# Latent projections ahead of the channel mixing in an attention and FFN kernel

## The chip, the cores and the metric

One core of one Trainium2 chip. The metric is the time of one execution on the device in microseconds, as the median of repeated runs. The profile is of one further execution.

## What is computed

`x` has shape (128, 32, 512): 128 samples, 32 channels, 512 time steps, in float32. The part of the reference that the change touches is the beginning:

```python
h  = einsum('bct,bcd->bdt', x, weights[condition])     # 16 sets of 32x32 channel weights
q_c = h @ Wq_c.T + bq_c                                # 192 latent features from 512 steps
kv  = h @ Wkv_c.T + bkv_c                              # 64 + 64 features
...                                                    # 32 heads, softmax over the 32 channels of a sample
x  = x + out                                           # then a gated convolution over time and a dequantised FFN
```

The channel mixing works on the channels of one sample, and the projection on its time steps. The two are linear and act on different axes, so they may be done in either order.

## The kernel before, in words

Five engines run instruction streams written out by hand and joined by semaphores. A queue runs strictly in the order of its code. The samples come in `NS` = 8 groups of 16, numbered 0 to 7 here (`k`). 16 samples of 32 channels make `ST` = 512 tokens. Each group is taken through two units `u` = 2k and 2k+1, one for each half of the 32 heads. In a unit, PE multiplies the latents by folded head weights (`fold`, L730, 64 rows in each half of the array), ACT takes the result to `qt`, PE makes the scores (L774), DVE and ACT do the softmax (`take_scores`, `below_max`, `soft`, `normalised`), and PE applies the probabilities (`values`, L797) and the value weights (`output`, L598 to L600).

The exact matmuls are built of three matmuls of type fp32r: a value is split into a rounded `high` part and a `low` rest, and `three` (L598 to L600) sums high*high, high*low and low*high. The split costs ACT a cast and DVE a subtraction. A few matmuls are plain fp32; each of them stands as two records in the trace.

A new group begins at the end of each odd unit, and this is the place of the change. `mixed_x(i)` (L616) mixes the channels of eight samples: the stationary operand is a tile of `x` (tokens by 128 time steps), the moving one a 128x128 block diagonal matrix `mix` of four samples' channel weights, in plain fp32, with the result laid out by time. It runs twice for a group, 16 matmuls of 128 columns. ACT and DVE split the result into `h_high` and `h_low` (`mixed_high`, `mixed_low`). Then `project_ca`, `project_ab` and `project_kv` each make 4 x 3 fp32r matmuls of 512 columns with the weights `wcT_high` and `wcT_low` as the stationary operand. ACT and DVE take the results out with their biases (`projected_ca`, `projected_ab`, `projected_kv`), and copies of 64 rows make the third latent tile `q_high[1]` and `q_low[1]`. PE's order there is output part 0, both `mixed_x`, output parts 1 and 2, the three projections, output part 3, and then `fold` of the next unit.

In units 1, 3 and 5 DVE has further work between these steps: `angles(first, last)`, steps of the convolution's angle computation on tiles of 512 elements (L1463 to L1484, `o_sum` in the trace). Seven of them stand beside each of the groups 1, 2 and 3, and none beside groups 4 to 7.

At the very start, DVE builds selection matrices (`chooser`) from the conditions, and PE makes the first channel weights from them (L915), and it turns the projection weights (L928), since `gather`, the indirect load of channel weights on POOL's queue, would come later. POOL's gathers serve group 1 onwards there.

## Time and profile before

| | us |
|---|---|
| median of 3 runs | 772.38 (770.73 to 773.88) |
| the profiled execution | 769.3 |
| its span in the profile | 767.5 |
| PE busy | 751.7 (98%) |
| DVE busy | 618.5 (81%) |
| ACT busy | 380.0 (50%) |
| POOL busy | 200.3 (26%) |

The profiled execution is 3.1 us below the median, and 1.8 us of it lie outside its span. Busy time on PE is counted while a matmul is in the array, with its fill and drain, so neighbouring matmuls overlap: what one costs is read from the distance between starts, and not from its duration. In the timeline the columns are start, duration, engine, line, operation, tiles and shape, and in brackets the idle time before and what ended it.

### The profile page before, as it was taken

What the parts mean: (1) busy time and instruction counts of PE and PEld (TensorE: products, weight loads), DVE (VectorE), ACT (ScalarE), POOL (GpSimd) and SP (SyncE); (2) the same over time, 40 slices, a digit from 0 to 9 for tenths busy, and PEclk for the clock granted to TensorE, in tenths of its full rate; (3) what the DMA queues carried; (4) which work ended last, traced back from release to release, by engine and by line L of the source; (5) the groups of instructions that cost most, each with busy time, mean ns of one, the idle gap of its engine ahead of it and who ended that gap; (6) DMA issues with size and microseconds to landing.
All of it is one profiled execution on the core that took longest, in us unless ns stands there. A gap on an engine that the chain in (4) does not pass through costs nothing.

```text
span 767.5 us, 18485 instructions
## 1 busy us (share of the span) xinstructions
PE 751.7 (98%) x7769; PEld 613.4 (80%) x7769; DVE 618.5 (81%) x1109; ACT 380.0 (50%) x675; POOL 200.3 (26%) x203
## 2 busy tenths in 40 slices
PE   9999999999999999999999999999999899999996
PEld 7777686978788787869787786978677699999996
DVE  5676899998998796777769776878889688888887
ACT  2475546546563675655465546545655322222221
POOL 5002020020002010270200000000040788888872
PEclk9999999999999999999999999999999999999999
DMA  9920010010001000000200010002207268888861
GB/s 223 229 76 5 2 59 3 1 59 3 2 2 59 2 1 29 1 4 14 87 1 2 2 56 2 1 2 59 84 2 187 69 142 209 200 208 204 205 132 70
DMA packets 42739, 51.74 MB, mean 67 GB/s; under 512 B 7025, under 2 KB 29601, under 8 KB 42657
## 3 DMA queue, kind: packets, MB, share of 16 engines
q1 hardware_dynamic: 40384, 49.87, 26.0%
q8 instruction: 62, 1.02, 0.6%
q0 software_dynamic: 1056, 0.49, 0.3%
q10 hardware_dynamic: 1216, 0.19, 0.2%
q14 instruction: 21, 0.16, 0.1%
HBM read 41.91 MB, written 8.63 MB: 66 GB/s over the span
## 4 chain that ended last, share of the span: by engine, by line
PE 92%; DVE 6%; ACT 1%; issue 1%; POOL 0%; DVEq 0%
PE ps L730 33%; PE ps L598 9%; PE ps L599 8%; PE ps L600 8%; PE ps L774 6%; PE ps L797 4%; PE ps L1087 4%; PE ps L616 4%; PE ps L1088 4%; PE ps L1056 2%; PE ps L693 1%; PE ps L1044 1%; PE ps L1046 1%; PE ps L1045 1%; PE ps L1070 1%
## 5 line engine op out<-in xcount | busy, mean ns | idle before, releaser
L1188 ACT ACTIVATE qt<-ps,m_bias 128x512 f32<-128x512 f32 x228 | 145.8, 686 | 97.0 <-PE ps L730 97.0
L730 PE MATMUL ps<-q_high,m_high 64*128 64x512 f32 x768 | 165.3, 397 | 0.5 <-issue 0.5
L730 PE MATMUL ps<-q_high,m_low 64*128 64x512 f32 x768 | 161.6, 387 | 0.0
L730 PE MATMUL ps<-q_low,m_high 64*128 64x512 f32 x768 | 113.8, 387 | 0.0
L730 PEld LDWEIGHTS ps<-q_high,m_high 64*128 64x128 f32 x768 | 88.9, 184 | 15.7 <-issue 6.2
L730 PEld LDWEIGHTS ps<-q_high,m_low 64*128 64x128 f32 x768 | 89.1, 184 | 8.9
L1450 DVE TENSOR_TENSOR z_low<-ps,z_high 128x512 fp32r<-128x512 f32 x128 | 79.5, 680 | 13.8 <-ACT z_high L1206 13.8
L730 PEld LDWEIGHTS ps<-q_low,m_high 64*128 64x128 f32 x768 | 81.3, 184 | 9.9
L528 POOL TENSOR_TENSOR o_sum<-o_part,o_part 128x512 f32<-128x512 f32 x7 | 9.1, 1304 | 288.5 <-ACT o_part L1216 288.5
L1193 ACT ACTIVATE sc<-sc 128x512 f32<-128x512 f32 x60 | 38.0, 633 | 76.3 <-DVE sc L1435 76.2
L1206 ACT CAST z_high<-ps 128x512 fp32r<-128x512 f32 x128 | 66.7, 597 | 12.3 <-PE ps L797 8.0
L1377 ACT COPY x1T_far<-ps 128x128 f32<-128x128 f32 x32 | 8.5, 267 | 103.7 <-PE ps L1056 103.7
L774 PE MATMUL ps<-qt,kv 128*32 128x512 f32 x480 | 55.0, 595 | 0.9 <-DVE z_low L1450 0.5
L598 PE MATMUL ps<-z_high,wvT_high 128*128 128x512 f32 (+1 forms) x132 | 53.5, 405 | 0.0
L599 PE MATMUL ps<-z_low,wvT_high 128*128 128x512 f32 (+1 forms) x132 | 51.0, 386 | 0.8 <-issue 0.8
L584 POOL TENSOR_TENSOR x_s<-x,fb 128x512 f32<-128x512 f32 x32 | 43.5, 1360 | 31.2 <-DVE x L1758 31.2
L600 PE MATMUL ps<-z_high,wvT_low 128*128 128x512 f32 (+1 forms) x132 | 50.7, 384 | 0.0
L1456 DVE TENSOR_SCALAR qt<-ps,m_bias 128x512 f32<-128x512 f32 x28 | 20.9, 749 | 35.1 <-PE ps L730 35.0
L1443 DVE TENSOR_TENSOR sc<-sc,row_stat 128x512 f32<-128x512 f32 x60 | 44.3, 738 | 2.1
L1445 DVE STREAM_TRANSPOSE pT<-sc 128x512 f32<-128x512 f32 x60 | 42.7, 712 | 2.0
L1435 DVE TENSOR_TENSOR sc<-sc,row_stat 128x512 f32<-128x512 f32 x60 | 41.6, 693 | 2.1
L576 POOL TENSOR_TENSOR x_s<-x_s,bo 128x512 f32<-128x512 f32 x32 | 41.9, 1310 | 0.0
(294 smaller groups left out, 1652.7 us busy)
## 6 DMA issues: line engine op xcount, KB each, us to landing
x_in<-in_x SPq DMA_DIRECT2D x16, 512.0 KB, 3.7
x_s<-in_x SPq DMA_DIRECT2D x32, 256.0 KB, 5.5
out<-res SPq DMA_DIRECT2D x31, 256.0 KB, 3.3
toep_high<-taps_scratch SPq DMA_DIRECT2D x32, 192.0 KB, 4.2
toep_low<-taps_scratch SPq DMA_DIRECT2D x32, 192.0 KB, 4.8
toep_far<-taps_scratch SPq DMA_DIRECT2D x32, 64.0 KB, 5.5
wq_nope<-in_L_attn_Wq_up SPq DMA_DIRECT2D x2, 768.0 KB, 10.8
wq_nope<-in_L_attn_Wq_up SPq DMA_DIRECT2D x1, 1536.0 KB, 18.1
```

Source lines behind the costliest of these rows:

```text
L576: pool.tensor_tensor(x_s[c % RX][:], x_s[c % RX][:], bo[:], ALU.add).then_inc(s["xb_done"], 1)
L584: pool.tensor_tensor(tiles(x_s[c % RX]), backwards(x1[c % 2]), tiles(fb), ALU.add).then_inc(s["x1b_done"], 1)
L598: pe.matmul(out, lh, rh, start=start, stop=False)
L599: pe.matmul(out, lh, rl, start=False, stop=False)
L600: return pe.matmul(out, ll, rh, start=False, stop=stop)
L730: mm = pe.matmul(ps[:, fold_bank(u, j) + e, :], weights[rows, (GH * g + j) // 2, c, :], moving[c][rows, :], start=start, stop=stop)
L774: mm = pe.matmul(ps[32 * b:32 * b + 32, SBANK[n], :], kv[:, tok], qt[:, :, tok], start=True, stop=True)
L1188: act.activation(qt[:, j, :], ps[:, fold_bank(u, j) + j % 2, :], ACT.Identity, bias=m_bias[:, h:h + 1]).then_inc(s["qt_done"], 1)
L1206: act.copy(z_part(z_high, m_, b), z_made(u, m_, b)).then_inc(s["zh_done"], 1)
L1443: dve.tensor_tensor(rows(n), rows(n), wide(n), ALU.mult).then_inc(s["norm_done"], 1)
L1445: dve.transpose(flat(pT[:, n]), flat(sc[:, n])).then_inc(s["turn_done"], 1)
L1450: dve.tensor_tensor(z_part(z_low, m_, b), z_made(u, m_, b), f(z_part(z_high, m_, b)), ALU.subtract).then_inc(s["zl_done"], 1)
```

## The change

Projection and mixing change places. `x` is given to the kernel laid out by time as well (`x_groups`: for each group, 128 partitions by 4 tiles of time by 512 tokens), and the projection weights are given transposed (`wcT`). ACT rounds the loaded `x` to `x_high`, and DVE makes `x_low`. `project(k)` then takes a tile of 128 tokens as the stationary operand and 320 columns of projection weights as the moving one, so for 4 token tiles, 4 time tiles and 3 products there are 48 fp32r matmuls of 320 columns. The 320 columns are all features once. ACT copies each result to `feat` in two pieces, the 320 columns and 64 of them a second time (`feat_taken`). `mix_features(k)` mixes over the channels: the stationary operand is 64 rows (two samples) of 128 features, the moving one 64 columns of channel weights, in plain fp32; for 3 parts, 4 token tiles and two row halves there are 24 matmuls, each half with a bank of its own. It waits for all four of `feat_taken`. The latents come out as before, in halves of a bank pair, and `kv` is taken out a unit later than before, after the third pair of latents.

At the start the selection matrices, their matmuls and the transposed weights go; `project_first` runs as the tiles of `x` arrive, and POOL gathers the channel weights of group 0 too, ahead of the small loads of the convolution's parameters.

```diff
+    x_low = [t(f"x_low{n}", [P, 2, ST], F32R, at=at) for n, at in enumerate((x_at, h_at + 4 * KB))]
+    x_raw = [t(f"x_raw{n}", [P, 2, ST], at=at) for n, at in enumerate((x_at, h_at + 4 * KB))]
+    x_high = t("x_high", [P, TT, ST], F32R, at=qt_at + 16 * KB)
+    feat = t("feat", [P, 4, 64 + FEAT], at=qt_at + 24 * KB)
...
+    mix = t("mix", [P, 4, 64], at=mix_at)
...
+    FEAT_BANK = (BS, BS + 1, BT + 1, BT)
...
+    def mixed_in(part):
+        if part == 0:
+            both = ps[:, BS:BS + 2, 0:256]
+        else:
+            both = ps[:, BZ:BZ + 2, 256 * (part - 1):256 * part]
+        return both
...
+            for tt in range(TT):
+                sp.dma_start(wcT_raw[:, tt, :], d["wcT"][:, tt, :]).then_inc(wc_in[tt], 16)
+                sp.dma_start(half_tile(x_raw, tt), d["x_groups"][0, :, tt, :]).then_inc(x_loaded[tt], 16)
...
+            def masked(k):
+                if k >= 1:
+                    pool.wait_ge(s["kv_ready"], k)
+                for j in range(2):
+                    pool.wait_ge(gather_in[j], 32 * (k + 1))
+                    pool.tensor_tensor(mix[:, 2 * j:2 * j + 2, :].rearrange("p g (b e) -> p g b e", b=2),
+                                       gathered[j][:].unsqueeze(2).broadcast_to([P, 2, 2, C]),
+                                       half_of[:].unsqueeze(1).unsqueeze(3).broadcast_to([P, 2, 2, C]),
+                                       ALU.mult).then_inc(s["mix_ready"], 1)
+            pool.wait_ge(s["row_ready"], 1)
+            gather(0)
+            gather(1)
...
+            def projected(k, n, tt, low):
+                left = half_tile(x_low, tt)[:, P * n:P * n + P] if low else x_high[:, tt, P * n:P * n + P]
+                out_n = ps[:, FEAT_BANK[n], 0:FEAT]
+                if low:
+                    return pe.matmul(out_n, left, wcT_high[:, tt, :], start=False, stop=(tt == TT - 1))
+                pe.matmul(out_n, left, wcT_high[:, tt, :], start=(tt == 0), stop=False)
+                return pe.matmul(out_n, left, wcT_low[:, tt, :], start=False, stop=False)
+            def project_first():
                 for tt in range(TT):
...
+                    pe.wait_ge(s["wcT_done"], tt + 1)
+                    pe.wait_ge(s["xh_done"], tt + 1)
+                    for n in range(4):
+                        projected(0, n, tt, False)
+                    pe.wait_ge(s["xl_done"], tt + 1)
+                    for n in range(4):
+                        mm = projected(0, n, tt, True)
+                        if tt == TT - 1:
+                            mm.then_inc(s["feat_ready"], 1)
+            def project(k):
+                u = 2 * k - 1
+                for n in range(4):
+                    if n != 2:
+                        pe.wait_ge(s["s_taken"], 4 * u + (1, 2, 0, 4)[n])
+                    else:
+                        pe.wait_ge(s["zl_done"], 8 * (u - 1) + 6)
+                    for tt in range(TT):
+                        if n == 0:
+                            pe.wait_ge(s["xh_done"], 4 * k + tt + 1)
+                        projected(k, n, tt, False)
+                    for tt in range(TT):
+                        if n == 0:
+                            pe.wait_ge(s["xl_done"], 4 * k + tt + 1)
+                        mm = projected(k, n, tt, True)
+                    mm.then_inc(s["feat_ready"], 1)
+            def mix_features(k):
+                pe.wait_ge(s["feat_done"], 4 * k + 4)
+                pe.wait_ge(s["mix_ready"], 2 * k + 2)
                 if k >= 1:
...
+                    pe.wait_ge(s["zl_done"], 8 * (2 * k - 1))
+                for part, made in enumerate(("q_ready", "qca_ready", "kv_ready")):
+                    for n in range(4):
+                        for h in range(2):
+                            rows = slice(64 * h, 64 * h + 64)
+                            mm = pe.matmul(mixed_in(part)[:, h, 64 * n:64 * n + 64], feat[rows, n, P * part:P * part + P],
+                                           mix[rows, n, :], start=True, stop=True)
+                    mm.then_inc(s[made], 1)
...
+            project_first()
...
                 output(u - 1, 0)
                 i = u + 1
                 if u % 2 == 1 and i < 2 * NS:
-                    mixed_x(i)
-                    mixed_x(i + 1)
                     output(u - 1, 1)
+                    project(i // 2)
                     output(u - 1, 2)
-                    project_ca(i // 2)
-                    project_ab(i // 2)
-                    project_kv(i // 2)
+                    mix_features(i // 2)
                     output(u - 1, 3)
...
+            def x_rounded(k, tt):
+                act.wait_ge(x_loaded[tt], 16 * (k + 1))
+                if k >= 1:
+                    act.wait_ge(s["s_ready"], 4 * (2 * k - 1) + 4)
+                act.copy(x_high[:, tt, :], half_tile(x_raw, tt)).then_inc(s["xh_done"], 1)
+            def feat_taken(k, n):
+                act.wait_ge(s["feat_ready"], 4 * k + n + 1)
+                act.copy(feat[:, n, 64:64 + FEAT], ps[:, FEAT_BANK[n], 0:FEAT])
+                act.copy(feat[:, n, 0:64], ps[:, FEAT_BANK[n], P:QL]).then_inc(s["feat_done"], 1)
+            def projected_ab(k):
                 if k == 0:
                     act.wait_ge(s["bias_in"], 16 * 6)
...
+                act.wait_ge(s["q_ready"], k + 1)
+                act.activation(by_halves(q_high[0]), mixed_in(0), ACT.Identity,
+                               bias=bq_c[:, 0:1]).then_inc(s["q_high_done"], 1)
+            def projected_ca(k):
+                act.wait_ge(s["kv_ready"], k + 1)
+                act.activation(by_halves(q_high[2]), mixed_in(1), ACT.Identity,
                                bias=bq_c[:, 1:2]).then_inc(s["q_high_done"], 1)
...
+            def crossed(k):
+                act.wait_ge(s["q_high_done"], 2 * k + 2)
                 act.copy(q_high[1][64:P, :], f(q_high[2][0:64, :])).then_inc(s["q_crossed"], 1)
...
                 act.copy(q_high[1][0:64, :], f(q_high[0][64:P, :])).then_inc(s["q_crossed"], 1)
             def projected_kv(k):
...
+                act.wait_ge(s["q_done"], 2 * k + 2)
+                act.activation(by_halves(kv), mixed_in(2), ACT.Identity, bias=bkv_c[:, 0:1]).then_inc(s["kv_done"], 1)
...
                         soft(u - 1, 3)
+                        projected_kv(u // 2)
...
                     latent(u // 2)
                 i = u + 1
                 if u % 2 == 1 and i < 2 * NS:
...
+                    for tt in range(TT):
+                        x_rounded(i // 2, tt)
+                    for n in range(3):
+                        feat_taken(i // 2, n)
+                        soft(u, n)
+                    feat_taken(i // 2, 3)
+                    projected_ab(i // 2)
                     projected_ca(i // 2)
...
+                    crossed(i // 2)
...
+            def x_rest(k, tt):
+                dve.wait_ge(s["xh_done"], 4 * k + tt + 1)
+                dve.tensor_tensor(half_tile(x_low, tt), half_tile(x_raw, tt), f(x_high[:, tt, :]), ALU.subtract).then_inc(s["xl_done"], 1)
...
+                    for tt in range(TT):
+                        x_rest(i // 2, tt)
                     angles(turn[0], turn[1])
-                    mixed_low(i)
-                    mixed_low(i + 1)
                     below_max(u, 0)
                     angles(turn[1], turn[2])
                     below_max(u, 1)
+                    angles(turn[2], turn[3])
+                    below_max(u, 2)
+                    below_max(u, 3)
+                    projected_ab(i // 2)
                     projected_ca(i // 2)
-                    below_max(u, 2)
-                    angles(turn[2], turn[3])
-                    projected_ab(i // 2)
-                    below_max(u, 3)
+                    crossed(i // 2)
...
+    laid["wcT"] = np.concatenate([q_c[64:], q_c[:64], kv_c]).reshape(FEAT, TT, P).transpose(2, 1, 0)
+    laid["x_groups"] = laid["x"].reshape(NS, 2, 4, 2, C, TT, P).transpose(0, 6, 5, 2, 1, 3, 4).reshape(NS, P, TT, ST)
```

How this moves ACT's queue in unit 5, where group 3 begins (`h_high`, `x_high` and `feat` are the steps of the new group, `sc` the softmax of unit 5). Before:

```order
L1206 CAST z_high<-ps 128x4x4x32 x5
L1128 CAST h_high<-ps 128x512 x4
L1193 ACTIVATE sc<-sc 128x512 x2
L1135 ACTIVATE q_high_70<-ps,columns 128x512
L1138 CAST q_high_69<-q_high_70 64x512
L1193 ACTIVATE sc<-sc 128x512
L1142 ACTIVATE q_high_68<-ps,columns 128x512
L1145 CAST q_high_69<-q_high_68 64x512
L1149 ACTIVATE kv<-ps,columns 128x512
```

And now:

```order
L1103 CAST x_high<-x_raw_67 128x512 x2
L1107 COPY feat<-ps 128x320
L1108 COPY feat<-ps 128x64
L1172 ACTIVATE sc<-sc 128x512
...
L1172 ACTIVATE sc<-sc 128x512
L1107 COPY feat<-ps 128x320
L1108 COPY feat<-ps 128x64
L1172 ACTIVATE sc<-sc 128x512
L1107 COPY feat<-ps 128x320
L1108 COPY feat<-ps 128x64
L1114 ACTIVATE q_high_70<-ps,columns 128x512
```

The fourth pair of feature copies, on which `mix_features` waits, now stands behind the third exponential of unit 5; before, no projection stood behind more than two of them, and each waited for PE alone.

DVE's queue in the same unit (`row_stat` and `sc<-sc,row_stat` are `below_max`, the `o_sum` rows are the angle steps). Before:

```order
L1429 STREAM_TRANSPOSE sc<-ps 128x512 x4
L1473 SCALAR_TENSOR_TENSOR o_sum<-o_sum 128x8x64 x2
L1402 TENSOR_TENSOR h_low<-ps,h_high 128x512 x4
L1433 TENSOR_REDUCE row_stat<-sc 128x16
L1435 TENSOR_TENSOR sc<-sc,row_stat 128x512
L1475 SCALAR_TENSOR_TENSOR o_sum<-quarter,o_sum 128x8x64
L1478 TENSOR_SCALAR o_sum<-o_sum 128x32x16
L1480 TENSOR_SCALAR o_sum<-o_sum 128x32x16
L1433 TENSOR_REDUCE row_stat<-sc 128x16
L1435 TENSOR_TENSOR sc<-sc,row_stat 128x512
L1409 SCALAR_TENSOR_TENSOR q_low_73<-ps,columns,q_high_70 128x512
```

And now:

```order
L1382 TENSOR_TENSOR x_low_65<-x_raw_67,x_high 128x512 x2
L1453 SCALAR_TENSOR_TENSOR o_sum<-o_sum 128x8x64 x2
L1413 TENSOR_REDUCE row_stat<-sc 128x16
L1415 TENSOR_TENSOR sc<-sc,row_stat 128x512
L1455 SCALAR_TENSOR_TENSOR o_sum<-quarter,o_sum 128x8x64
...
L1413 TENSOR_REDUCE row_stat<-sc 128x16
L1415 TENSOR_TENSOR sc<-sc,row_stat 128x512
L1462 TENSOR_TENSOR o_sum<-o_sum 128x8x64
L1464 TENSOR_SCALAR o_sum<-o_sum 128x8x64
L1413 TENSOR_REDUCE row_stat<-sc 128x16
L1415 TENSOR_TENSOR sc<-sc,row_stat 128x512
```

The subtraction for the new group comes first, and all seven angle steps stand ahead of the third `sc<-sc,row_stat`, for which ACT's third exponential waits.

## Rows read from the trace of the kernel before

**Rows 1.** The page: busy time, and the granted clock in 40 slices

```profile
PE 751.7 (98%) x7769; PEld 613.4 (80%) x7769; DVE 618.5 (81%) x1109; ACT 380.0 (50%) x675; POOL 200.3 (26%) x203
...
PEclk9999999999999999999999999999999999999999
```

**Rows 2.** The chain in order of time: start us, us, what

```profile
111.07 14.53 PE ps L730 x126
...
232.51 3.57 PE ps L616 x32
...
248.33 14.53 PE ps L730 x126
...
301.14 3.57 PE ps L616 x32
```

**Rows 3.** Timeline of PE, group 1: start us, us, engine line op

```profile
95.06 1.95 PE L616 MATMUL ps<-mix,x_in 128*128 128x128 f32 x16
...
98.55 0.48 PE L598 MATMUL ps<-z_high,wvT_high 128*128 128x512 f32 x1
...
101.38 0.39 PE L598 MATMUL ps<-h_high,wcT_high 128*128 128x512 f32 x1
...
109.54 0.39 PE L598 MATMUL ps<-z_high,wvT_high 128*128 128x512 f32 x1
```

**Rows 4.** Timeline of PE, last stage: 384 and 256 columns

```profile
607.38 0.34 PE L598 MATMUL ps<-x1T_high,toep_high 128*128 128x384 f32 x1
...
607.92 0.28 PE L598 MATMUL ps<-x1T_high,toep_high 128*128 128x256 f32 x1
...
652.83 0.28 PE L1087 MATMUL ps<-wfT_a,y_high 128*128 128x256 f32 x1
...
653.79 0.40 PE L1044 MATMUL ps<-woT_high,o_high 128*128 128x512 f32 x1
```

**Rows 5.** The chain in order of time: matmuls on part of the rows

```profile
36.73 1.54 PE ps L693 x48
...
86.43 1.14 PE ps L797 x63
```

**Rows 6.** Timeline of PE, group 3: where the array is divided anew

```profile
230.85 0.50 PE L598 MATMUL ps<-z_high,wvT_high 128*128 128x512 f32 x1
...
247.94 0.39 PE L600 MATMUL ps<-z_high,wvT_low 128*128 128x512 f32 x1
...
248.26 0.50 PE L730 MATMUL ps<-q_high,m_high 64*128 64x512 f32 x2
```

**Rows 7.** Timeline of DVE, group 3 (unit 5)

```profile
230.53 2.50 DVE L1429 STREAM_TRANSPOSE sc<-ps 128x512 f32<-128x512 f32 x4
...
232.96 1.37 DVE L1473 SCALAR_TENSOR_TENSOR o_sum<-o_sum 128x512 f32<-128x512 f32 x2
...
237.34 0.68 DVE L1433 TENSOR_REDUCE row_stat<-sc 128x16 f32<-128x512 f32 x1
...
238.66 0.69 DVE L1475 SCALAR_TENSOR_TENSOR o_sum<-quarter,o_sum 128x512 f32<-128x512 f32 x1
...
240.36 0.69 DVE L1433 TENSOR_REDUCE row_stat<-sc 128x16 f32<-128x512 f32 x1
```

**Rows 8.** Timeline of ACT, group 3

```profile
238.78 0.63 ACT L1193 ACTIVATE sc<-sc 128x512 f32<-128x512 f32 x1 [2.08 <-DVE sc L1435]
```

**Rows 9.** Timeline of PE and DVE, group 1

```profile
93.56 0.50 PE L598 MATMUL ps<-z_high,wvT_high 128*128 128x512 f32 x1
...
96.55 0.65 DVE L1463 TENSOR_TENSOR o_sum<-parT,pos 128x512 f32<-128x512 f32 x1
```

**Rows 10.** Timeline of the start: POOL, SP's queue, PE's weight loads

```profile
12.31 0.98 POOL L467 DMA_INDIRECT gathered<-in_L_cond_weights,row_of  x1 [0.31 <-issue]
...
15.04 1.54 SPq L364 DMA_DIRECT2D taps_scratch<-zero  x3
...
29.17 0.55 PEld L674 LDWEIGHTS ps<-wq_nope,wk 128*64 128x64 f32 x8 [1.02 <-DMA wq_rope<-in_L_attn_Wq_up]
```

More of the change, by code:

```diff
@@ L288, in build @@
     s = {n: mem.sem(n) for n in weight_names + attention_names + taps_names + ffn_names + channel_names}
+    wc_in = [mem.sem(f"wc_in{n}") for n in range(TT)]
+    x_loaded = [mem.sem(f"x_loaded{n}") for n in range(TT)]
     gather_in = [mem.sem(f"gather_in{n}") for n in range(2)]
@@ L322, in build, with half_tile, by_halves @@
     th_of = lambda hs: theta[:, hs, :].rearrange("p h (x c) -> p h x c", x=4)
-    def x_arrived(i):
-        return s[("x_loaded", "x1_loaded")[i % 2]], 16 * (i // 2 + 1)
-    def mix_of(i):
-        return mix if i % 2 == 0 else mix_first if i == 1 else mix_odd
-    x_v = d["x"].rearrange("(g b) c t -> (b c) g t", b=4)
+    def half_tile(pair, tt):
+        return pair[tt // 2][:, tt % 2, :]
+    def mixed_in(part):
[4 more added lines that the diff above has]
+        return both
+    def by_halves(tile):
+        return tile[:].rearrange("p (h x) -> p h x", h=2)
     def tiles(tile):
@@ L457, in _ @@
             pool.wait_ge(s["ident_ready"], 2)
-            for b in range(4):
-                rows = slice(32 * b, 32 * b + 32)
-                pool.memset(set_of[rows, :], float(b)).then_inc(s["delta_ready"], 1)
-                pool.tensor_copy(delta[rows, :], ident[rows, rows]).then_inc(s["delta_ready"], 1)
             def gather(i):
-                if i >= 4:
+                if i >= 2:
                     pool.wait_ge(s["mix_ready"], i - 1)
@@ L545, in front @@
             def front(u):
-                front_begun(u)
-                front_ended(u)
+                if u % 2 == 0 and u + 2 < NU:
+                    masked(u // 2 + 1)
+                    if u + 4 < NU:
+                        gather(u + 4)
+                        gather(u + 5)
                 if u % 2 == 0 and u >= 2:
@@ L600, in three @@
                 return pe.matmul(out, ll, rh, start=False, stop=stop)
-            def mixed_x(i):
-                pe.wait_ge(*x_arrived(i))
-                pe.wait_ge(s["mix_ready"], i + 1)
-                if i >= 2 and i % 2 == 0:
-                    pe.wait_ge(s["zl_done"], 8 * (i - 2) + 7)
-                elif i >= 2:
-                    pe.wait_ge(s["s_taken"], 4 * (i - 2) + 2)
-                elif i == 1:
-                    pe.wait_ge(s["wcT_done"], 2)
-                for n in range(2):
-                    for t_ in range(2):
-                        for g in range(2):
-                            tt = 2 * n + t_
-                            o = t_ * HT + g * P
-                            mm = pe.matmul(ps[:, MIX_BANK(i, n), o:o + P], x_in[i % 2][:, g, tt * P:(tt + 1) * P],
-                                           mix_of(i)[:, g, :], start=True, stop=True)
-                    mm.then_inc(s["h_ready"], 1)
@@ L740, in by_high @@
                     for c in (0, 2, 1):
+                        if c == 2 and g == 0 and j == 0:
+                            pe.wait_ge(s["q_high_done"], 2 * k + 2)
                         if c == 1 and g == 0 and j == 0:
@@ L747, in by_low @@
                     if g == 0 and j == 0:
+                        pe.wait_ge(s["q_done"], 2 * k + 1)
+                    both(j, m_high, q_low, 0)
+                    if g == 0 and j == 0:
                         pe.wait_ge(s["q_done"], 2 * k + 2)
-                    both(j, m_high, q_low, 0)
                     both(j, m_high, q_low, 2)
@@ L909, in turned_wo @@
                 mm.then_inc(s["woT_ready"], 1)
-            def first_mixing(i):
-                for g in (2 * i, 2 * i + 1):
-                    pe.wait_ge(s["chooser_ready"], g + 1)
-                    for k in range(4):
-                        mm = pe.matmul(ps[:, CHOSEN_BANK[i], C * g:C * g + C], chooser[g][:, k, :], cond_w[:, k, :],
-                                       start=(k == 0), stop=(k == 3))
-                    mm.then_inc(s["first_mix"], 1)
             pe.wait_ge(s["busy_ready"], 1)
@@ L1241, in _ @@
             act.copy(warm[:], ones[:])
[L1242 to L1247 removed]
+            for tt in range(TT):
+                act.wait_ge(wc_in[tt], 16)
+                act.copy(wcT_high[:, tt, :], wcT_raw[:, tt, :]).then_inc(s["wcT_high_done"], 1)
+                x_rounded(0, tt)
+            for n in range(4):
+                feat_taken(0, n)
+            projected_ab(0)
             projected_ca(0)
[L1249 removed]
+            crossed(0)
             lat_taken(0)
@@ L1664, in _ @@
                         dve.wait_ge(s["ssm_const"], 5)
+                    for tt in range(TT):
+                        x_rest(i // 2, tt)
                     angles(turn[0], turn[1])
-                    mixed_low(i)
-                    mixed_low(i + 1)
                     below_max(u, 0)
```

237 lines of the change are left out of this document (52 added, 185 removed).

## The prediction

> **What bounds the kernel now.** I read the page first, then the chain of work that ended last, then the timelines of PE, DVE and ACT around the place of the change. PE is busy for 98% of the span and its granted clock is full in every slice [rows 1]. The chain runs through PE: a group's `mixed_x` starts at 232.51, the fold after it at 248.33, and the next group's `mixed_x` at 301.14, a period of 68.6 us [rows 2]. So in the middle of the kernel a microsecond less on PE is a microsecond less in all, as long as nothing makes PE wait. The reader should see two things in the rows: what the replaced matmuls cost PE, by the distance of their starts, and how little room DVE's queue has at that place.
>
> **What goes from PE.** In a group from 1 on, the 16 plain fp32 matmuls of `mixed_x` take from 95.06 to 98.55, 3.49 us. The 36 matmuls of 512 columns take from 101.38 to 109.54, 8.16 us or 0.227 each [rows 3]. Together 11.65 us.
>
> **What comes, the projection.** There are 48 matmuls of 320 columns, with a new stationary operand of 128 columns before each. The trace has no 320 columns. It has 384 columns at (607.92 - 607.38)/3 = 0.180, and 256 columns, with as many rows of weights loaded, at (653.79 - 652.83)/8 = 0.120 [rows 4]. These are the bounds, 5.8 and 8.6 us. I take the middle, 0.149 by the slope between 256 and 512 columns (0.120 to 0.227) and 0.150 by the nearer pair: 0.149 x 48 = 7.15 us. The Trainium skill ("TensorE: Matmul & The Clock Gate", section "Back-to-back issue gap") gives N/2.4 + 2.5 ns for an isolated stream, and so 0.136 for 320 columns and 6.5 us. The rows stand against it where weights are loaded each time: its 0.109 for 256 columns is 0.120 here. By its figure the sum below would be 2.6 us better.
>
> **What comes, the mixing.** There are 24 plain fp32 matmuls, 48 records, each with a weight load of 64 rows by 128 columns and only 64 moving columns. The load sets the pace, and the question is whether the two row halves load and run side by side. A full-array record of L616 (128 columns loaded) costs 3.49/32 = 0.109 [rows 3]. Side by side the 48 records cost 24 x 0.109 = 2.6 us, one behind the other 5.2 us. For side by side speak L693, whose 64x64 pieces in two row halves go at 1.54/48 = 0.032, and L797, whose 32-row pieces go at 1.14/63 = 0.018 [rows 5]. If every load waited for the one before, at half the columns of L616's, they would cost 0.055 each. I take 2.65 us.
>
> **What comes, the divided array.** Where PE goes from full rows to parts of the array and back, the trace shows extra time: the fold's first pair starts 0.32 after the last full matmul instead of 0.227 [rows 6], and the first full matmul after the scores takes 0.50 where one in the middle takes 0.39 [rows 6]. With both parts that is some 0.2 us for each crossing. The change adds two crossings in a group (into the mixing, and out to output part 3). The bounds are 0 and 0.7 us; I take 0.45. The Trainium skill ("TensorEngine Tiling (Array Packing)", section "Key Properties") says that a change of tiling mode drains TensorE; the trace agrees, with these 0.1 and 0.11 us.
>
> PE's sum for a group is 7.15 + 2.65 + 0.45 = 10.25 us against 11.65, a gain of 1.4. In groups 4 to 7 I take 0.1 off for the first `x_low` tiles. DVE's four transposes of scores end at 230.53 + 2.45 = 233.0 in group 3 [rows 7], and four subtractions of about 0.61 end at 235.45. PE reaches the first low products at 233.7 + 8 x 0.149 = 234.9 and the fourth tile at 235.4, so it waits about 0.1. **Groups 4 to 7 gain 1.3 each, 5.2 us.** ACT's casts there are hidden: it has been idle, starts as the last scores are done at about 231.0, and four casts of some 0.55 us end at 233.3, before output part 1 ends at 230.85 + 1.5 + 1.37 = 233.7. So are the feature copies: ACT's exponential of 512 columns takes 0.63 [rows 8], so a pair of 320 and 64 columns costs about 0.6, and the last pair ends 0.6 to 0.9 us after the projection, under output part 2 with its 6 x 0.228 = 1.37 us. If that cover were gone, PE would wait those 0.9 us.
>
> **The added wait, groups 1 to 3.** `mix_features` waits for the fourth pair of copies, which stands on ACT behind the third exponential, which waits on DVE for three `below_max` and all seven angle steps. For group 3 in the times of the old trace: x_low done 235.45; two steps 1.4 (232.96 to 234.36, 1.37 busy [rows 7]); `below_max` 1.32 (237.34 to 238.66 [rows 7]); three steps 1.7 (238.66 to 240.36 [rows 7]); `below_max` 1.32; two steps 1.2; `below_max` 1.4 with its tail. That makes 243.8. The exponential of 0.63 [rows 8] ends at 244.5, the copies at 245.1. PE has done output part 2 at 233.7 + 7.15 + 0.1 + 1.4 = 242.4 and waits 2.7 us. Then 2.65 of mixing, 0.25 of crossing, 1.37 of output part 3 and 0.1 put the fold at 249.5, where it stood at 248.3: **group 3 loses 1.2.** ACT's and DVE's latents (0.7 us each, the crossing copies 0.6) follow in the shadow of output part 3 and of the fold's first products, so no further wait. Group 2 has a cheaper set of seven steps (about 3.6 us instead of 4.3) and **loses about 0.5**. In group 1 output part 0 starts at 93.56, but DVE's transposes end only at 96.55 [rows 9], 3.0 us behind PE instead of 2.2. The same sum from there: 99.0 + 1.8 + 1.32 + 1.7 + 1.32 + 1.4 + 1.4 = 107.9, copies done at 109.2, fold at 113.5 against 111.0 [rows 2]: **group 1 loses 2.5.** Behind these waits the next unit simply starts later; nobody else is late, as its softmax has a whole fold to end in.
>
> **The start.** PE loses the selection matmuls, the turned weights and their waits. But its first fold hung on a DMA: the third set of weight products found its `wq` tiles only at 29.17 [rows 10]. They are in one queue behind `x` and the projection weights, which shrink by 0.13 MB; that is worth about 0.7 us, and the rest of the earlier end of the projection is hidden by it. **The start gains 0.7** (bounds: -3 and +2).
>
> **The sum.** 5.2 + 0.7 - 1.2 - 0.5 - 2.5 = 1.7 us less. Against the profiled execution, 769.3 (span 767.5), that is 767.6; this execution stands 3.1 below the median, so against the median of 772.4 I forecast 770.7. About 0.5% (3.9 us) is what a measurement of this kernel can tell from no change, and 1.7 us lies within.
>
> **The rivals.**
>
> *All groups gain.* If the third exponential comes sooner than I sum, or the copies are not behind it, groups 1 to 3 gain like the others: 7 x 1.3 + 0.7 = 9.8 us, 762.6. The order of both queues speaks against it, and the old rows show that DVE has no idle time between its transposes and the second `below_max` but for waits on h. It would show as no idle time ahead of the mixing. 12%.
>
> *The halves do not run side by side.* Then the mixing costs 5.2 us, in seven groups 2.6 x 7 = 18 us more, and the time is 789: slower. The point from which it decides is 0.072 us for a record (0.055 forecast): above it, 336 records in groups 1 to 7 cost 3.9 + 1.7 us more. For it: no row has halves of 128 loaded columns and few moving ones; the fold's have 512 moving columns to hide a load. Against it: rows 5. The Trainium skill has a rule that speaks this way ("TensorE: Matmul & The Clock Gate", section "LDWEIGHTS (loading the stationary operand)"): a load's time goes by its columns, whatever the rows, so halving the rows and doubling the loads saves nothing unless the halves overlap. 11%.
>
> *The start is late.* POOL now issues four gathers of about 1.3 us (0.98 and 0.31 idle [rows 10]) before its small loads and before it clears the tile of zeros, for which SP's queue waits ahead of the second set of `wq` loads; by the gathers and the five loads after them the clearing moves to about 14.4 us, and SP got there at 15.04 [rows 10]. Where it comes after SP, the `wq` tiles and the first fold are late by as much. Price up to 3 us against my 0.7: 774. 12%.
>
> **How the numbers follow.** My forecast has 62%; its unknowns (0.149 by +-0.008 over four groups +-1.5, the crossings +-1.5, the stalls +-1.5, the start +-1, the runs' own spread +-1.5) give about 768 to 774 on their own, with 15 of the 62 points faster than 0.5%, 45 within it and 2 slower. All groups gaining adds 12 to faster, serial halves 11 to slower, the late start 7 to within and 5 to slower; 3 are left for what I don't see, 1 faster and 2 slower. Faster 0.28, within 0.5% 0.52, slower 0.20. The range of 8 in 10 runs from 762 to 776; it leaves out the serial halves.
>
> **What would show it.** Right: records of the projection 0.15 apart; 24 mixing matmuls in 2.7 us; PE idle for 2 to 4 us ahead of the mixing in groups 1 to 3, with ACT's exponential behind DVE as the cause, and no such idle in groups 4 to 7; periods from fold to fold 1.3 shorter in the latter. Wrong: mixing at 5 us; idle ahead of the mixing in every group, which would mean that the copies, and not the angle steps, are late; idle ahead of the first low product; a first fold after 32 us; or a granted clock below full after one of the new waits. A fold slower than 14.53/7 = 2.08 us a pair of heads [rows 2] would mean that `kv`, now taken out by ACT between the fold's first results, holds up the banks.

## The result and the profile after

Both kernels were timed in turn on one chip, four executions each. Before: 771.74 us (770.73 to 773.88). After: **781.18 us** (776.98 to 784.91). The ratio is 1.012, with a 95% interval of 1.0066 to 1.0173: slower, and outside the predicted range. On the chip of experiments 1 to 8 the same changed kernel took 775.3 us against 769.56, a ratio of 1.0093 (1.0064 to 1.0122). The executions of the changed kernel also lie further apart, 8 and 7 us against 3 and 2. Ratios leave out executions that were disturbed, so one can stand a little below that of the medians.

The profiled execution after took 779.11 us, with a span of 777.3 against 767.5. The page of after shows that PE is less busy than before and that its granted clock is no longer full in every slice; it answers to [rows 1]:

```profile
PE 747.4 (96%) x7949; PEld 614.6 (79%) x7949; DVE 613.3 (79%) x1100; ACT 393.3 (51%) x740; POOL 201.8 (26%) x201
...
PEclk9699998999999899999999999999999999999999
```

So the change took work from PE, as meant, and the time still grew. Where it grew is read from the starts of the fold (L730 before, L723 after). The table has the distances between them in the two traces and in three of the experiments that follow. Unit 1 is the second fold; "group 1" is the distance from the fold of unit 1 to the first fold of group 1, and so on.

| us | before | after | after, matmuls in the waits | after, copy ahead | before, two waits added |
|---|---|---|---|---|---|
| start to fold of unit 1 | 65.9 | 71.3 | 70.1 | 65.1 | 66.6 |
| to group 1 | 45.1 | 50.4 | 47.2 | 44.9 | 49.5 |
| to group 2 | 68.6 | 69.0 | 69.0 | 67.2 | 68.7 |
| to group 3 | 68.6 | 71.8 | 69.7 | 67.5 | 71.1 |
| to group 4 | 68.6 | 68.3 | 67.3 | 67.3 | 68.7 |
| to group 7 (three groups) | 208.2 | 204.0 | 204.0 | 204.0 | 208.2 |
| to the end | 242.4 | 242.5 | 241.5 | 247.5 | 242.9 |

After against before, that is +5.4 at the start, +5.3, +0.3 and +3.2 in groups 1 to 3, -0.3 in group 4 and -4.2 in groups 5 to 7 (differences here and below are taken before rounding).

The chain of waits of after, at group 1, in order of time (start us, us, what):

```profile
111.56 0.70 DVE row_stat L1413
...
112.28 0.70 DVE sc L1415
...
113.00 0.63 ACT sc L1172
113.63 0.32 ACT feat L1107
113.95 0.12 ACT feat L1108
...
114.11 5.08 PE ps L634 x48
119.19 0.72 PE ps L584
119.91 0.43 PE ps L585
...
121.78 0.43 PE ps L723
```

This is the forecast wait: row maxima on DVE, exponential on ACT, fourth copy on ACT, mixing on PE. What the forecast did not have is the length of what comes behind it. The timelines of after show the mixing of groups 1, 2, 3 and 4, the same 48 records each time, with the wait before them in brackets:

```profile
114.11 5.08 PE L634 MATMUL ps<-mix,feat 64*128 64x64 f32 x48 [2.53 <-ACT feat L1108]
...
186.27 2.90 PE L634 MATMUL ps<-mix,feat 64*128 64x64 f32 x48 [1.65 <-ACT feat L1108]
...
255.97 3.70 PE L634 MATMUL ps<-mix,feat 64*128 64x64 f32 x48 [2.37 <-ACT feat L1108]
...
326.34 2.90 PE L634 MATMUL ps<-mix,feat 64*128 64x64 f32 x48
```

The stretches of after explain it (columns: PE, PEld, DVE, ACT and POOL busy, then PEclk, DMA share, GB/s). They are two in the start, the mixing and output part 3 of group 1, the same of group 2, and of group 3 the end of the mixing, part 3 and the first pairs of the fold:

```profile
18.90:29.10 10.20, 6.69 (x76) 5.18 (x74) 5.66 (x21) 3.78 (x6) 2.43 (x5) 0.50 1.08 225
36.00:39.40 3.40, 3.40 (x20) 2.92 (x18) 2.68 (x12) 1.05 (x3) 0.00 (x0) 0.50 1.09 243
114.50:121.30 6.80, 6.80 (x51) 6.29 (x50) 2.07 (x3) 2.61 (x4) 1.75 (x3) 0.50 0.07 26
186.30:190.70 4.40, 4.40 (x56) 3.81 (x56) 1.65 (x3) 2.12 (x4) 1.30 (x3) 1.00 0.34 124
257.90:264.60 6.70, 6.70 (x34) 5.15 (x34) 4.66 (x8) 1.92 (x3) 4.08 (x5) 0.50 0.02 5
```

Behind the two longer waits PE ran at 0.50 of its clock (1.2 instead of 2.4 GHz) for 6.8 us each time; behind the one of 1.65 us it kept full clock, and group 2 came out as forecast. That gives the theory: **the waits of 2.37 and 2.53 us are paid twice, once as idle time and once as a slow clock for the work behind them.** The rivals are that the waits alone are the loss and the clock hardly matters, that the small 64-by-64 matmuls and not the waits make the clock fall, and that the start is the main loss.

The start itself, in the timeline of after:

```profile
18.04 0.69 ACT L1114 ACTIVATE q_high<-ps,columns 128x512 fp32r<-128x512 f32 x1 [1.43 <-PE ps L634]
...
20.32 1.55 PE L666 MATMUL ps<-wq_nope,wk 128*64 128x193 f32 x8 [0.30 <-issue]
...
22.68 0.69 ACT L1119 ACTIVATE q_high<-ps,columns 128x512 fp32r<-128x512 f32 x1 [3.96 <-remote]
...
25.09 0.91 PE L686 MATMUL ps<-ident,lat 64*64 64x64 f32 x12 [3.21 <-ACT lat L1139]
...
30.34 0.88 PE L666 MATMUL ps<-wq_nope,wk 128*64 128x193 f32 x8 [0.99 <-DVE m_bias L1474]
```

PE had finished the mixing by 20.0, and went on to L666 at 20.32; ACT took up L1119 only at 22.68, with nothing in the trace that releases it. PE then waited 3.2 us for ACT's copy of `lat` and stood at half clock in between.

Every timed execution has its mean granted clock on record, whether it has a trace or not. It is 0.998 to 1.000 for the kernel before in the experiments and 0.972 to 0.989 in the eight executions of the changed one; the profiled one has 0.982. So the low clock is no accident of this one trace: five of the other seven executions have more of it.

### The profile page after: what moved, and what is told of

It is laid out like the page before. It is cut to its first block, busy times and chain, and to the rows that moved or that the text cites. A ratio compares the mean times of both kernels' runs of the same rounds, so it can differ in the third digit from the quotient of the medians.

```text
span 777.3 us, 18935 instructions
## 1 busy us (share of the span) xinstructions
PE 747.4 (96%) x7949; PEld 614.6 (79%) x7949; DVE 613.3 (79%) x1100; ACT 393.3 (51%) x740; POOL 201.8 (26%) x201
## 4 chain that ended last, share of the span: by engine, by line
PE 83%; DVE 12%; ACT 2%; issue 1%; DMA 1%; another core or an unknown queue 1%; POOL 0%; SPq 0%; DVEq 0%; ACTq 0%
PE ps L723 33%; PE ps L584 6%; PE ps L771 5%; PE ps L585 5%; PE ps L586 5%; PE ps L794 4%; PE ps L1062 4%; PE ps L1063 4%; PE ps L634 3%; PE ps L1031 2%; DVE z_low L1430 2%; PE ps L592 2%; PE ps L593 2%; PE ps L594 2%; PE ps L686 1%
## 5 line engine op out<-in xcount | busy, mean ns | idle before, releaser
L723 PE MATMUL ps<-q_high,m_high 64*128 64x512 f32 x768 | 168.6, 401 | 1.2 <-issue 1.2
L723 PE MATMUL ps<-q_high,m_low 64*128 64x512 f32 x768 | 164.2, 390 | 0.0
L723 PE MATMUL ps<-q_low,m_high 64*128 64x512 f32 x768 | 115.1, 388 | 0.0
L723 PEld LDWEIGHTS ps<-q_high,m_high 64*128 64x128 f32 x768 | 91.5, 186 | 16.8 <-issue 7.5
L723 PEld LDWEIGHTS ps<-q_high,m_low 64*128 64x128 f32 x768 | 91.6, 186 | 8.6
L723 PEld LDWEIGHTS ps<-q_low,m_high 64*128 64x128 f32 x768 | 82.9, 185 | 9.4
L470 POOL TENSOR_TENSOR mix<-gathered,half_of 128x128 f32<-128x128 f32 x16 | 6.1, 399 | 216.4 <-PE ps L634 208.8
```

Of the source, the lines that this page charges most:

```text
L723: mm = pe.matmul(ps[:, fold_bank(u, j) + e, :], weights[rows, (GH * g + j) // 2, c, :], moving[c][rows, :], start=start, stop=stop)
```

## The experiments

Experiments 1 to 8 ran on one chip, 9 and 10 on another. All times are against the kernel before on the same chip, 769.4 to 769.85 us there. Each kernel was also profiled once.

**1. Matmuls in the waits.** A fill-in of 14 matmuls ahead of the mixing in groups 1 and 3, into a bank that nobody reads then:

```
 output(u - 1, 2)
+if i // 2 in (1, 3):
+    for _ in range(14):
+        pe.matmul(ps[:, BX, 0:FEAT], x_high[:, 0, 0:P], wcT_high[:, 0, :], start=True, stop=True)
 mix_features(i // 2)
```

> The changed kernel with 14 matmuls of 320 columns (fp32r, into a free bank, 14 x 0.146 = 2.0 us) put behind the third block of the output projection, where TensorE waits 2.5 and 2.4 us for the fourth copy of the latents in groups 1 and 3; nothing that waits is released earlier. Theory (the granted clock falls to 1.2 GHz behind these two waits and charges the work after them): the two half-clock stretches at 114.5 and 257.9 us are gone, the mixing of group 1 takes 2.9 instead of 5.08 us and that of group 3 2.9 instead of 3.70, the output block and the fold behind them run at full pace, and the time falls by 4 to 5 us from the changed kernel's. Rival (the waits alone are the loss): no change within 1 us. Second rival (the fillers delay the mixing): slower by up to 1 us.

Measured: 769.88 us, ratio 1.0006 (0.9988 to 1.0025), so 5.4 us below the changed kernel's 775.3 on that chip. The mixing in groups 1 and 3 of its timeline:

```profile
112.91 2.90 PE L638 MATMUL ps<-mix,feat 64*128 64x64 f32 x48 [0.49 <-ACT feat L1113]
...
251.57 2.90 PE L638 MATMUL ps<-mix,feat 64*128 64x64 f32 x48 [0.33 <-ACT feat L1113]
```

No copy comes earlier in this kernel: the mixing of group 1 starts 42.8 us behind the fold of unit 1 in both traces, that of group 3 65.3 us behind the fold of group 2. Yet the mixing takes 2.90 instead of 5.08 and 3.70 us, and the granted clock is full in both groups. By the table, 3.2 us came back in group 1, 2.1 in the way to group 3 and 1.0 behind it, 6.3 in all. That is what the slow clock charged in the profiled execution. What is left, +2.1, +0.3 and +1.1 in groups 1 to 3, is the waits less the saved work.

**2. The copy ahead of the exponential.** ACT takes the fourth copy before its third exponential:

```
-for n in range(3):
+for n in range(2):
     feat_taken(i // 2, n)
     soft(u, n)
+feat_taken(i // 2, 2)
 feat_taken(i // 2, 3)
+soft(u, 2)
```

> The changed kernel with ScalarE's fourth copy of the latents put ahead of its third exponential in every group behind the first, so that it no longer waits for VectorE's row maxima and angle steps. Theory (that order makes the waits, and the waits make the slow clock): TensorE's waits before the mixing shrink from 2.5, 1.65 and 2.4 us to about 0.4, no half-clock stretch remains in groups 1 and 3, and each of the three groups gains as groups 4 to 7 do, about 1.3 us: 13 us less than the changed kernel, 767 to 769 us, so faster than before by 3 to 5 us. Rival (the third exponential, now late, holds the values of its unit): the gain is half of that, 774 us.

Measured: **760.68 us, ratio 0.9877** (0.9852 to 0.9902), 14.6 us below the changed kernel. Group 1 of its timeline:

```profile
104.55 0.41 ACT L1107 COPY feat<-ps 128x320 f32<-128x320 f32 x1
...
104.95 0.44 ACT L1107 COPY feat<-ps 128x320 f32<-128x320 f32 x1
...
105.56 2.90 PE L634 MATMUL ps<-mix,feat 64*128 64x64 f32 x48 [0.20 <-ACT feat L1108]
106.78 0.63 ACT L1172 ACTIVATE sc<-sc 128x512 f32<-128x512 f32 x1 [1.28 <-DVE sc L1417]
107.32 0.67 ACT L1114 ACTIVATE q_high<-ps,columns 128x512 fp32r<-128x512 f32 x1
```

The exponential has lost nothing: DVE is done with its rows only then, while ACT stood idle for it 1.28 us. The waits are 0.2 us, the clock is full in the groups, and groups 2 and 3 now gain 1.4 and 1.1 like the later ones. Group 1 gains only 0.3; 0.4 us of it goes to waits for `x_low`, and the rest I did not trace. The gain was more than expected, 14.6 against 13 us. The start of this kernel is that of the changed one, so the order in the groups alone makes this difference. The mean granted clock of its four executions is 0.991 to 0.996, where the changed kernel has 0.974 to 0.989 on this chip.

**3. The first bias copy ahead of DVE's chain at the start.**

```
+bias_part(0)
 exp_begun(dve, chain, log_in[:], ek[:], ep[:])
 exp_ended(dve, chain, log_in[:], ek[:], ei[:], ep[:])
-bias_part(0)
```

> The changed kernel with the first bias copy of VectorE (out of the latent bank) moved ahead of its chain of some 20 small steps on the state-space parameters at the start. In the trace the third set of products starts at 30.34 us behind that copy, which sat behind the chain. Theory (VectorE's chain, started late by ScalarE's late second rounding at 22.68 us, sets the first fold): the first fold starts 1.5 to 2.5 us earlier than 34.2 us and the time falls by as much. Rival (TensorE's own pauses behind instruction loading, or the chain now holding m_low, set it): under 0.7 us.

Measured: 777.32 us, ratio 1.0067 (1.0036 to 1.0099), with ten executions from 768.5 to 785.8 us. No gain over the changed kernel's 1.0093 can be told from that. In its profile the first fold starts at 29.0 us, and PE no longer waits for `m_bias` ahead of it. But kernels whose start is that of the changed one have the first fold anywhere from 29.4 us (experiment 8) to 34.2 (after) and 35.8 (experiment 1), so one profile can't tell what the order gives there. What it gives is lost at a later wait, in this timeline row:

```profile
42.41 0.88 PE L666 MATMUL ps<-wq_nope,wk 128*64 128x193 f32 x8 [1.82 <-DMA wq_rope<-in_L_attn_Wq_up]
```

The fold of unit 1 starts at 65.2, about where it does in experiment 2 (65.1) and before (65.9). In this profile the weights that arrive hold it.

**4. The wait alone, in the kernel before.** The kernel before with

```
 project_ab(i // 2)
+if u in (1, 5):
+    pe.wait_ge(s["exp_done"], 4 * u + 3)
 project_kv(i // 2)
```

> The kernel before, with one wait added and nothing else: ahead of the projection to keys and values of groups 1 and 3 TensorE waits for the third exponential of the unit. It isolates the wait from the mixing and the latents. Theory: TensorE stands 1.5 to 2.5 us in each, the granted clock falls behind at least one of the two, and the loss is larger than the sum of the waits: 5 to 9 us slower than before. Rival (a wait of this length costs itself and no more, the clock fell in the changed kernel for its small matmuls of 64 by 64): the granted clock stays full and the loss is the 3 to 4 us of the waits.

Measured: 775.46 us, ratio 1.0076 (1.0058 to 1.0094), 6.1 us slower. Its stretches, the first wait, what follows it, the second wait, what follows it:

```profile
107.70:110.50 2.80, 0.02 (x2) 0.02 (x1) 2.67 (x6) 0.74 (x3) 0.00 (x0) 0.89 0.00 0
110.50:113.00 2.50, 2.50 (x6) 2.02 (x7) 2.40 (x4) 1.12 (x2) 0.00 (x0) 0.50 0.00 0
249.40:251.60 2.20, 0.00 (x0) 0.00 (x0) 2.10 (x5) 0.68 (x2) 0.00 (x0) 1.00 0.00 0
251.60:255.00 3.40, 3.39 (x15) 2.83 (x16) 3.09 (x6) 1.49 (x3) 0.00 (x0) 1.00 0.01 2
```

The wait of 2.78 us was followed by half clock and cost 4.4 us (49.5 - 45.1). The one of 2.22 us was not and cost 2.5 (71.1 - 68.6). There is no 64-by-64 matmul of the mixing here, so a wait is enough to bring the clock down. (Whether such matmuls can do it too is another question, on which experiment 10 bears.) The four executions lie within 2.4 us and all have a granted clock of 0.998, so most of this kernel's loss of 6.1 us is the two waits themselves, 5.0 us.

**5. The changed kernel again,** on the chip of experiments 1 to 8.

> The changed kernel itself, on the chip of the experiments, so that they have their own measure: before took 769.4 us there and 771.7 where the change was timed. Expected 777 to 780 us. Theory on its start: it is not steady, since three of its waits there hang on transfers and on ScalarE's pause of 2.7 us, which two of the experiments did not show; so runs that differ by 5 us or more, where those of before lie within 3 us.

Measured: 775.3 us (772.37 to 779.32), below the expected 777 to 780. In its profile, the fastest of the four, unit 1 starts at 66.4 and group 1 at 115.2, with half clock for 3.4 us in group 1 instead of 6.8. The same waits (2.54, 1.66, 2.38 us) are thus not followed by the same slow stretch in every execution, and so the kernel's times spread.

**6. Both orders together** (experiments 2 and 3).

> Both orders together: the fourth copy of the latents ahead of the third exponential, and the first bias copy ahead of VectorE's chain at the start. Theory: the first alone gave 760.7 us, with the first fold at 30.8 us and that of unit 1 at 65.1; the second alone had the first fold at 29.0 but lost it again to a wait of 1.8 us for the second part of the query weights, and stood at 65.2 at unit 1. So the start is held by the weights that arrive, and the two together give no more than the first: 759 to 761 us. Rival (the order at the start is worth its 1.8 us where the clock holds): 758 to 759 us.

Measured: 761.47 us, ratio 0.9886 (0.9863 to 0.9909). As the theory had it, no more than experiment 2.

**7. Both orders, and the start kept busy.** DVE takes copies 1 and 3 at the start, and PE runs 4 of the matmuls of experiment 1 ahead of the first mixing and 4 behind the first products.

> As the kernel with both orders, and at the start alone: VectorE takes two of the four copies of the latents (half of 1.9 us), and TensorE runs 4 matmuls of 320 columns ahead of the mixing and 4 behind the first products, where it stands still. Theory of the clock: no half-clock stretch before the first fold, and the first fold 1 to 2 us earlier than without; by the weights that arrive most of it is given back before unit 1: 757 to 760 us. Rival (instruction and gather transfers make the start unsteady whatever the engines do): runs spread over 5 us as before and the median does not move.

Measured: **759.8 us, ratio 0.9882** (0.9865 to 0.99), executions from 758.98 to 761.61. Its profile has full clock up to 755.8 us, the first fold at 29.1 and unit 1 at 64.4; ahead of the first fold PE waits 2.2 us for `wq_rope`. The median is that of experiments 2 and 6 within their intervals.

**8. The angle steps out of the way instead.** ACT's order as in the change, but DVE's angle steps of units 1, 3 and 5 done ahead of the heads of units 2, 4 and 6.

> The changed kernel with ScalarE's order as it is, but VectorE's angle steps of groups 1 to 3 (7, 6 and 7 of them) moved into the next unit, so that they don't stand between the row maxima. It asks whether VectorE alone made the wait. Theory: the third exponential then comes 3 us earlier in these groups, TensorE's waits before the mixing go from 2.5 and 2.4 us to below 0.5, no half clock in groups 1 and 3, and the time falls by 8 to 10 us, less what the steps cost in their new place (up to 1 us a unit, as they stand ahead of heads that VectorE rounds): 768 to 773 us. Rival (ScalarE's own order is the wait): under 3 us of gain.

Measured: 771.6 us, ratio 1.0025 (1.0006 to 1.0043). That is 3.7 us below the changed kernel, where 8 to 10 were expected less up to 1 us a unit. The wait before the mixing is gone in groups 1 to 3, so DVE's steps alone did make it. But in unit 2 its timeline has

```profile
127.87 0.69 DVE L1443 TENSOR_TENSOR o_sum<-parT,pos 128x512 f32<-128x512 f32 x1
...
129.32 0.75 DVE L1436 TENSOR_SCALAR qt<-ps,m_bias 128x512 f32<-128x512 f32 x1
...
131.53 1.20 PE L794 MATMUL ps<-pT,ctok 32*64 32x128 f32 x64 [3.66 <-DVE z_low L1430]
```

PE waits 3.66 us there and 2.66 in unit 4, and both are followed by 3.4 us of half clock. I had priced the moved steps at up to 1 us a unit; they cost a whole wait. The wait had moved, not gone.

**9. The start's three edits alone,** with the groups as changed.

> The changed kernel with the three edits at its start alone (first bias copy ahead of VectorE's chain, two of the four latent copies on VectorE, 4 and 4 matmuls of 320 columns where TensorE stands still) and its order in the groups as it was. With it the account of the loss can be closed. Theory: the start of the changed kernel costs between nothing and 5 us from run to run, the groups 1 to 3 the steady rest. The first fold at 29 to 30 us and unit 1 at 64 to 65.5 us, runs closer together than the 7 us of the changed kernel, and a median of 771 to 774 us: 2 to 4 below its 775.3, and the groups' 12 to 14 us above the kernel with both orders remain. Rival (the start is the main loss): 766 us or less.

Measured: 776.12 us (768.62 to 776.66), ratio 1.0073 (1.0049 to 1.0096). Expected were 771 to 774; the median did not move from the 775.3 of experiment 5. The profiled execution is the fastest of the five, with a granted clock of 0.992, and its start is even 1.4 us shorter than before. The other four took 772.7 to 776.7 us at 0.981 to 0.988, and no trace shows where. With experiment 2, which gained 14.6 us without a change to the start, this says that the start is not where the lasting loss is.

**10. The halves one after the other.** Experiment 2's kernel with

```
-for n in range(4):
-    for h in range(2):
+for h in range(2):
+    for n in range(4):
```

> The kernel with the fourth copy ahead of the third exponential, and in the mixing the two 64-row halves one after the other: four matmuls of rows 0 to 63, then four of rows 64 to 127, instead of one of each in turn. It prices the rival of the prediction that the halves don't run side by side. Theory: what runs together is neighbours in the queue on different halves, at 0.112 us a pair; grouped, only one pair in eight stays together, and the mixing of a group takes 4.5 to 5.3 instead of 2.9 us: 2 us in each of seven groups, 14 to 16 us in all, so 775 us and again slower than before. Rival (the pitch belongs to the single matmul, whatever stands beside it): no change from 760.7.

Measured: 767.95 us, ratio 0.9981 (0.9953 to 1.001), 7.3 us slower than experiment 2 on the other chip. Its timeline in groups 1 and 5:

```profile
105.69 3.87 PE L634 MATMUL ps<-mix,feat 64*128 64x64 f32 x48 [0.21 <-ACT feat L1108]
...
381.62 3.61 PE L634 MATMUL ps<-mix,feat 64*128 64x64 f32 x48
...
385.58 0.63 PE L585 MATMUL ps<-z_low,wvT_high 128*128 128x512 f32 x1
```

The stretches of the mixing in group 5 and of what follows it, in the columns used above:

```profile
381.60:385.20 3.60, 3.60 (x50) 3.52 (x49) 0.75 (x1) 0.69 (x1) 0.00 (x0) 1.00 0.79 270
385.40:388.70 3.30, 3.30 (x10) 2.16 (x11) 2.59 (x5) 1.78 (x3) 2.85 (x4) 0.50 0.04 10
```

At full clock the mixing takes 3.6 instead of 2.9 us. That is 0.7 more in each of seven groups, 5.0 in all. In this profile the way from unit 1 to group 7 is 8.0 us longer than in experiment 2. The other 3.0 us stand behind the mixing of groups 1 and 5, where PE ran at half clock for 3.4 us each time; the 3.87 us above hold the first of it. PE had waited 0.21 us ahead of the one and not at all ahead of the other. So the rival of the small matmuls is not refuted for this order of the halves: twice in seven groups they were followed by half clock without a wait of note. With the halves in turn, as in the changed kernel, this happened in none of the nine profiles: there a mixing of groups 1 to 7 was followed by half clock only where PE had waited 1.66 us or more ahead of it.

Expected were 4.5 to 5.3 us. The single starts in its trace show why it is less: records of one half follow each other at 0.11 us, but those of the other half, queued behind them, start before the first four are through, so much of the overlap survives.

## Why the prediction was wrong

**PE's sum in groups 4 to 7 was right.** Forecast: 1.3 each, 5.2 in all. Measured: 4.2 in three groups, and 1.4 in group 4 once the slow clock of 1.0 us behind group 3 is taken out: 5.5 before rounding. Within it, the 48 projections follow each other at about 0.147 us (forecast 0.149) and the mixing takes 2.90 with its last record's tail of about 0.2 (forecast 2.65). These rows of after show the first pitch:

```profile
108.27 0.31 PE L593 MATMUL ps<-wcT_high,x_high 128*128 128x320 f32 x1
108.42 0.31 PE L594 MATMUL ps<-wcT_low,x_high 128*128 128x320 f32 x1
108.57 0.31 PE L593 MATMUL ps<-wcT_high,x_high 128*128 128x320 f32 x1
```

The rival of serial halves is refuted by the 2.90 us, and experiment 10 shows that in turn is the better order, by 0.7 us a group.

**The waits were right in place, cause and length.** Forecast for group 3: 2.7 us, measured 2.37, behind the same links in the same order. At full clock, in experiment 1, groups 1 to 3 lost 2.1, 0.3 and 1.1 us, where 2.5, 0.5 and 1.2 were forecast. Only group 2's wait of 1.65 us lies outside the 2 to 4 us that were named as the sign of being right.

**The step that failed is the price of a wait.** The added-wait part summed each group as idle time plus work at full pace, and ended "group 1 loses 2.5" and "group 3 loses 1.2". The granted clock stood only in the last paragraph, as something that could show the forecast wrong, with no price and no chance. It was a mechanism that the forecast waits themselves would set off. In the profiled execution it charged 3.2 us in group 1 and 3.1 behind the wait of group 3 (experiment 1). The forecast could have bounded it: work that follows the wait takes twice as long while the clock is low, and 4.4 us of mixing and output part 3 stand right behind each wait, so 0 to 4.4 us in each of groups 1 to 3. With half of the upper bound the forecast would have read 777, still below the 781.2 that was measured. The Trainium skill ("TensorE: Matmul & The Clock Gate", section "HAM oscillation — how this bites in real kernels") describes a kernel that drops to the low clock in each wait for a transfer and pays for it in the matmuls behind. This case's stretches agree, at 0.50 behind waits of 2.53 and 2.37 us; the waits in that section's example are longer, 3 to 5 us, and here shorter ones were enough.

**The start was sized wrong for the profiled execution.** Forecast: a gain of 0.7, bounds -3 and +2. The profiled execution lost 5.4 to unit 1, outside them; experiment 1 lost 4.3. In the other profiles of kernels with this start or an eased one unit 1 stands at 64.4 to 66.4 us, against 65.9 before. The rival of a late start put the cause on POOL's order, which would hold up the second set of `wq` loads; that was not it, as they were issued at 16.38 us, and at 16.61 before. In the profile of after the trace shows ACT's pause of 2.7 us and the half clock around PE's waits; in experiment 1 it shows a wait of 3.85 us for POOL's `mix`, which itself waited for a gather, and 17.1 us of half clock.

Term by term, the profiled execution lies 11.5 us above the forecast (its span grew by 9.8 where 1.7 less was forecast): 6.1 at the start, 2.8 and 2.0 in groups 1 and 3, 1.0 on the way to group 4, and -0.3 in the rest. In this execution the start missed by as much as the clock in the groups. That the price of the wait is the step that failed for the median rests on experiments 2 and 9: the order in the groups gave 14.6 us with the start as it was, and an eased start gave nothing. What the start costs in executions without a trace stays open.

**The rival "all groups gain", 762.6, is the kernel of experiment 2.** It was to come true if the copies were not behind the exponential. With that order the time is 8.7 us below before on its chip, where the rival had 9.8.

## What to carry to other kernels

Where PE is the bound, price a new wait of some 2.5 us on it by the wait and the work behind it at half pace, not by its length alone, and give the second part a chance of its own. When a copy that PE waits for shares an engine with work that itself waits, look at the order on that engine first: here one swapped line was worth 14.6 us, and turned a slower kernel into one that is 1.2% faster than before. Moving the offending work elsewhere can only move the wait.

## What the runs showed that was not expected

- The clock's fall is not steady. Waits of 2.53 to 2.54 us in group 1 were followed by half clock for 6.8 us in one execution and 3.4 in three others (experiments 3, 5 and 9). The wait of 1.65 in group 2 was not followed by one in four profiles out of five, and in experiment 3 by 6.8 us. The changed kernel and experiments 3, 8 and 9, which have such waits, spread by 7 to 17 us, before by 2 to 5 and experiment 7 by 2.6. But the waits alone don't make the spread: experiment 4 has two and spread by 2.4, experiment 1 has them filled in groups 1 and 3 and spread by 7. Experiment 10 spread by 10.5 at granted clocks of 0.984 to 0.995, the fastest execution with the highest, in keeping with the half clock behind some of its mixings.
- PE and ACT pause with no releaser in the trace. In experiment 2's profile, the slowest of its four executions, PE stood still in the last values product:

```profile
586.99 1.01 PE L839 MATMUL ps<-pT_last,ctok 32*64 32x64 f32 x42 [2.90 <-issue]
```

  It was followed by 6.8 us of half clock, and the table's last row shows the cost, 5 us. Experiments 6 and 8 had the same pause (2.64 and 3.73 us), and the other profiles at that place 0.9 us or less. A transfer of instructions lies inside the pause; for the stretch 584 to 587 us the list of DMA queues has

```profile
q1 hardware_dynamic: 438, 0.52, 55.2%
q8 instruction: 1, 0.02, 2.1%
```

  and there is one in ACT's pause at the start of after too. In experiment 7's profile, without the pause, the transfer starts at 580.24 us, 4.5 us earlier. But each profile has 63 such transfers, most of them in no pause. That the pause waits for it is a guess that no run here tests.
- Output part 3 and the fold, which the change doesn't touch, ran at half pace as well: the slow clock is charged to whatever comes next.
